# Residual sums on TensorE and LayerNorm statistics on ScalarE beside a clipped recurrence

## The reference

```python
h = ln(x, g1, b1);  real, imag = split(h @ W_to.T)
def step((sr, si), (r, i)):                 # 1024 steps, one after the other
    sr = sr * decay + r * 0.1;  si = si * decay + i * 0.1
    nr = clip(sr * c - si * s, -10, 10);  ni = clip(sr * s + si * c, -10, 10)
x2 = x + 0.1 * (scan_out @ W_from.T)
y  = x2 + 0.1 * (gelu(ln(x2, g3, b3) @ W1.T + b1) @ W2.T + b2)
x  = norm(y)                                                     # "layer 2" below
x  = norm(x + softmax(q(x) k(ctx)^T / 4) v(ctx) @ Wo.T + bo)     # "layer 3", 16 heads, 154 keys
```

## Time and profile before

| | us |
|---|---|
| median of 3 runs | 2178.86 (2178.73 to 2180.55) |
| the profiled execution's own time | 2181.41 |
| its span, first to last instruction | 2179.6 |
| last recurrence step ends | 603 |
| the stage of the change ends | 693 |

### The profile page before, as it was taken

How to read it: one execution, slowest core, us unless ns; L and a number is a source line. 1 busy time by engine, 2 the same in 40 slices (tenths; PEclk the granted TensorE clock), 3 DMA queues, 4 the chain that set the end, 5 groups by cost and what they waited for, 6 DMA issues and landing times.

```text
span 2179.6 us, 34541 instructions
## 1 busy us (share of the span) xinstructions
PE 1758.3 (81%) x12713; PEld 1265.2 (58%) x12713; DVE 1469.8 (67%) x5012; ACT 992.0 (46%) x2312; POOL 500.8 (23%) x602
## 2 busy tenths in 40 slices
PE   3546666766677877999999999999888999998808
PEld 1335555655564335566666766666657999983306
DVE  3788887787822587677777567776735666753695
ACT  2524334443343753455555345555315445543762
POOL 3011112111120012333333333333302333320002
PEclk9767788878787986999999999999999999999959
DMA  5000000000000011100000000000403333310001
GB/s 153 1 0 1 1 1 1 1 1 1 1 1 1 1 39 24 60 1 1 1 1 1 1 1 2 1 1 2 128 1 88 88 88 78 70 30 0 0 0 39
DMA packets 86314, 49.82 MB, mean 23 GB/s; under 512 B 40205, under 2 KB 83905, under 8 KB 85953
## 3 DMA queue, kind: packets, MB, share of 16 engines
q1 hardware_dynamic: 79361, 47.05, 8.3%
q10 hardware_dynamic: 6784, 0.56, 0.3%
HBM read 45.50 MB, written 2.10 MB: 22 GB/s over the span
## 4 chain that ended last, share of the span: by engine, by line
PE 60%; DVE 19%; ACT 9%; issue 3%; POOL 3%; POOLq 0%; DVEq 0%; ACTq 0%
PE PS L1526 6%; PE PS L1553 6%; PE PS L1824 5%; PE PS L1540 5%; PE PS L713 3%; PE PS L1511 3%; PE PS L1501 3%; DVE sq L667 3%; DVE nx L664 3%; PE PS L719 3%; PE PS L2237 3%; PE PS L1887 2%; PE PS L1568 2%; PE PS L1843 2%; PE PS L1493 2%
## 5 line engine op out<-in xcount | busy, mean ns | idle before, releaser
L1680 POOL TENSOR_SCALAR px<-px,crl 128x128 f32<-128x128 f32 (+7 forms) x128 | 225.9, 1765 | 420.6 <-DVE crl L1652 420.6
L1591 ACT ACTIVATE px<-PS,cnm 128x128 f32<-128x128 f32 (+7 forms) x256 | 189.5, 741 | 265.3 <-DVE cnm L1637 258.5
L182 POOL TENSOR_SCALAR rstd<-mv 128x1 f32<-128x1 f32 x128 | 41.5, 325 | 794.3 <-DVE mv L161 793.6
L667 DVE TENSOR_SCALAR sq<-nx 128x4 f32<-128x4 f32 x1024 | 186.0, 182 | 35.3 <-DVE nx L664 0.2
L664 DVE TENSOR_TENSOR_SCAN nx<-sq 128x6 f32<-128x6 f32 x1024 | 176.2, 172 | 35.5 <-SPq L2304 2.3
L1634 DVE TENSOR_REDUCE cm<-PS 128x1 f32<-128x128 f32 (+6 forms) x224 | 154.2, 689 | 56.9 <-PE PS L1526 56.4
L1540 PE MATMUL PS<-ident,px 128*128 128x128 f32 x1152 | 159.8, 280 | 13.3 <-ACT qT L1579 9.6
L1540 PEld LDWEIGHTS PS<-ident,px 128*128 128x128 f32 x1152 | 131.2, 142 | 60.6 <-issue 35.3
L1526 PE MATMUL PS<-kT,qT 64*128 64x512 f32 (+3 forms) x768 | 158.9, 519 | 4.5 <-ACT px L1591 2.6
L1553 PEld LDWEIGHTS PS<-pT,V 128*64 128x64 f32 x2304 | 124.1, 137 | 64.0 <-issue 34.6
L1553 PE MATMUL PS<-pT,V 128*64 128x128 f32 x2304 | 154.1, 278 | 6.4 <-DVE pT L1645 2.8
(11 more groups left out here) (318 smaller groups left out, 3830.3 us busy)
## 6 DMA issues: line engine op xcount, KB each, us to landing
xbs<-in_fside_Bx16xSxS SPq DMA_DIRECT2D x8, 1232.0 KB, 6.6
fsrc<-in_fside_Bx16xSxS SPq DMA_DIRECT2D x8, 1232.0 KB, 6.6
xmk<-in_mask_Bx16xSxS_bk SPq DMA_DIRECT2D x8, 308.0 KB, 8.5
fsrc<-in_mask_Bx16xSxS_bk SPq DMA_DIRECT2D x8, 308.0 KB, 8.3
X<-in_x SPq DMA_DIRECT2D x1, 2048.0 KB, 11.8
w<-in_L_attn_W_ffn SPq DMA_DIRECT2D x2, 1024.0 KB, 11.9
t<-in_L_ffn_w SPq DMA_DIRECT2D x2, 1024.0 KB, 11.3
out<-xs SPq DMA_DIRECT2D x16, 128.0 KB, 1.7
```

Of the source, the lines that this page charges most:

```text
L667: e.tensor_scalar(o, bass.AP(k.nx, 2, [[6, P], [0, 2], [3, 2]]), 10.0, -10.0, ALU.min, ALU.max).then_inc(sem("rec.clip"), 1)
L1591: e.activation(k.px[n % 2][:, h, 0:width], src, ACT.Exp, scale=-1.0, bias=k.cnm[:, n % 4, h:h + 1], accum_out=k.cl[:, n % 4, h:h + 1]).the ...
L1680: e.tensor_scalar(k.px[n % 2][:, 0, 0:width], k.px[n % 2][:, 0, 0:width], k.crl[:, n % 4, 0:1], None, ALU.mult).then_inc(sem("c.normal0"), 1)
```

## The change

For L = 1 and 2 in blocks 0 to 6, and for L = 3 in blocks 0 to 5 (`aside`), VectorE has no part in the norm any more. TensorE adds the residual by one more matmul into the same PSUM tile, with the identity, or ten times the identity where ScalarE scales the sum by 0.1 afterwards (`ident10`). ScalarE copies the sum from PSUM to `r4` and accumulates it (`sum`), forms the negative mean (`mean`), squares the deviations and accumulates them (`square`); GpSimd forms the reciprocal root from that (`root`), and ScalarE forms the shift and applies both (`shift`, `side`). The last blocks take the path of the other layers: residual, statistics and the application (`unit`) on VectorE. The numbers between the steps change: for L1 and L2 the step `shift` comes 7 and the turn 11 recurrence steps behind `sum`, where the turn came 7 behind `r`; for L3 it is 16 and 4. GpSimd's two additions to X move from the residual and the down steps to the turn and the up steps. Shown without unchanged lines; the new tiles and their reservation are left out.

```diff
...
+def aside(L, T):
+    return T % BT < {1: BT - 1, 2: BT - 1, 3: BT - 2}.get(L, 0)
+def taken(k, L, T):
+    return ("ln.act", k.ln_act["sum", L, T]) if aside(L, T) else ("ln.r", k.order.at("r", L, T))
...
     def unit(L, T):
-        if L == 0:
+        if L in (0, 1):
-        dst = k.xs4[:, lane, :] if L in (0, 7) else k.xt(T)
+        dst = k.xs4[:, lane, :] if L in (0, 1, 7) else k.xt(T)
...
-    def shift(L, T):
-        rs = k.rstd[:, lane_of(L, T), :]
-        w.wait_ge("ln.rstd", at("aggr", L, T))
-        e.tensor_scalar(rs[:, 0:1], k.mv[:, lane_of(L, T), 0:1], rs[:, 1:2], -1.0, ALU.mult, ALU.mult).then_inc(sem("ln.shift"), 1)
-    return {"aggr": aggr, "shift": shift}
+    def root(L, T):
+        s, rs, n = k.lst[:, lane_of(L, T), :], k.rstd[:, lane_of(L, T), :], 2 * at("root", L, T)
+        w.wait_ge("ln.act", k.ln_act["square", L, T])
+        e.tensor_scalar(rs[:, 0:1], s[:, 2:3], 1.0 / D, 1e-5, ALU.mult, ALU.add).then_inc(sem("ln.root"), 1)
+        w.wait_ge("ln.root", n - 1)
+        e.tensor_tensor(rs[:, 1:2], rs[:, 0:1], k.neghalf[:, :], ALU.pow).then_inc(sem("ln.root"), 1)
+    return {"aggr": aggr, "root": root}
...
     def turn(L, T):
-        if L in (1, 2):
+        if aside(L, T):
...
 def norm_scalar(e, w, k):
+    def total(L, T):
+        lane, b, t = lane_of(L, T), T // BT, T % BT
+        if L == 3:
+            n = at("n.query", T)
+            w.wait_ge("n.out", n)
+            ps = k.PS[:, 2 + n % 2, D:2 * D]
+        else:
+            if L == 1:
+                w.wait_ge("net.from", at("from", 1, t))
+            else:
+                w.wait_ge("net.down", at("down", 1, t))
+            ps = k.PS[:, 0, b * D:(b + 1) * D]
+        e.activation(k.r4[:, lane, :], ps, ACT.Identity, scale=1.0 if L == 3 else 0.1, accum_out=k.lst[:, lane, 0:1]).then_inc(sem("ln.act"), 1)
+    def mean(L, T):
+        s, n = k.lst[:, lane_of(L, T), :], k.ln_act["sum", L, T]
+        w.wait_ge("ln.act", n)
+        e.mul(s[:, 1:2], s[:, 0:1], -1.0 / D).then_inc(sem("ln.act"), 1)
+    def square(L, T):
+        n, lane = at("square", L, T), lane_of(L, T)
+        w.wait_ge("ln.act", k.ln_act["mean", L, T])
+        w.wait_ge("ln.act", k.ln_junk[n - 1])
+        e.activation(k.ljunk[:, :], k.r4[:, lane, :], ACT.Square, bias=k.lst[:, lane, 1:2], accum_out=k.lst[:, lane, 2:3]).then_inc(sem("ln.act"), 1)
+    def shift(L, T):
+        s, rs = k.lst[:, lane_of(L, T), :], k.rstd[:, lane_of(L, T), :]
+        w.wait_ge("ln.root", 2 * at("root", L, T))
+        e.mul(s[:, 3:4], s[:, 1:2], rs[:, 1:2]).then_inc(sem("ln.act"), 1)
     def side(L, T):
-        w.wait_ge("ln.shift", at("shift", L, T))
+        w.wait_ge("ln.act", k.ln_act["shift", L, T])
-        e.activation(dst, k.r4[:, lane, :], ACT.Identity, scale=k.rstd[:, lane, 1:2], bias=k.rstd[:, lane, 0:1]).then_inc(sem("ln.side"), 1)
+        e.activation(dst, k.r4[:, lane, :], ACT.Identity, scale=k.rstd[:, lane, 1:2], bias=k.lst[:, lane, 3:4]).then_inc(sem("ln.side"), 1)
...
-    return {"side": side, "put": put}
+    return {"sum": total, "mean": mean, "square": square, "shift": shift, "side": side, "put": put}
...
-        needs["n.query", T] = [("put", 2, T)] + ([("r", 3, k.near_tiles[n - 2])] if n > 1 else [])
+        needs["n.query", T] = [("put", 2, T)] + ([("sum" if aside(3, k.near_tiles[n - 2]) else "r", 3, k.near_tiles[n - 2])] if n > 1 else [])
-        needs["r", 3, T] = [("n.out", T)]
+        needs["sum" if aside(3, T) else "r", 3, T] = [("n.out", T)]
...
     def norm(L, gap):
-        for kind, wait in (("r", gap), ("stats", 0), ("aggr", 0), ("shift", 0), ("side", 5), ("turn", 2), ("put", 0)):
+        beside = (("sum", gap), ("mean", 0), ("square", 0), ("root", 0), ("shift", 7), ("side", 0), ("turn", 4))
+        alone = (("r", gap), ("stats", 0), ("aggr", 0), ("unit", 0), ("turn", 0))
+        for kind, wait in (*(beside if aside(L, t) else alone), ("put", 0)):
...
+            w.wait_ge("ln.side", at("side", 2, T - 1))
...
-        e.matmul(k.PS[:, 0, b * D:(b + 1) * D], k.zs[:, b, :], k.wfT[:, :], start=True, stop=True).then_inc(sem("net.from"), 1)
+        y = e.matmul(k.PS[:, 0, b * D:(b + 1) * D], k.zs[:, b, :], k.wfT[:, :], start=True, stop=not aside(1, t))
+        if aside(1, t):
+            w.wait_ge("tails", 2)
+            y = e.matmul(k.PS[:, 0, b * D:(b + 1) * D], k.ident10[:, :], k.xt(b * BT + t), start=False, stop=True)
+        y.then_inc(sem("net.from"), 1)
...
     def down(b, t):
-            m = e.matmul(k.PS[:, 0, b * D:(b + 1) * D], k.hT[:, j, b, :], k.W2T[:, j, :], start=j == 0, stop=j == 7)
+            m = e.matmul(k.PS[:, 0, b * D:(b + 1) * D], k.hT[:, j, b, :], k.W2T[:, j, :], start=j == 0, stop=j == 7 and not aside(2, t))
+        if aside(2, t):
+            w.wait_ge("net.bias", at("down", b, t))
+            m = e.matmul(k.PS[:, 0, b * D:(b + 1) * D], k.ident10[:, :], k.xt(b * BT + t), start=False, stop=True)
...
+        e.mul(k.ident10[:, :], k.ident[:, :], 10.0).then_inc(sem("tails"), 1)
...
-    def r(L, T):
+    def turn(L, T):
-            w.wait_ge("ln.r", at("r", L, T))
+            w.wait_ge(*taken(k, L, T))
-    def down(b, t):
-        w.wait_ge("net.added", at("down", b, t))
-        e.tensor_tensor(k.xt(b * BT + t), k.xt(b * BT + t), k.b2s[:, :], ALU.add).then_inc(sem("net.bias"), 1)
-    return {"tern_round": tern_round, "rec_in": rec_in, "r": r, "down": down}
+    def up(t, b):
+        if b < B:
+            w.wait_ge("net.added", at("down", b, t))
+            e.tensor_tensor(k.xt(b * BT + t), k.xt(b * BT + t), k.b2s[:, :], ALU.add).then_inc(sem("net.bias"), 1)
+    return {"tern_round": tern_round, "rec_in": rec_in, "turn": turn, "up": up}
...
 def near_ends(T):
-    yield 20, ("r", 3, T)
-    yield 1, ("stats", 3, T)
-    yield 1, ("aggr", 3, T)
-    yield 0, ("shift", 3, T)
-    yield 6, ("side", 3, T)
+    if aside(3, T):
+        for kind, wait in (("sum", 16), ("mean", 0), ("square", 0), ("root", 0), ("shift", 4), ("side", 0)):
+            yield wait, (kind, 3, T)
+    else:
+        for kind, wait in (("r", 20), ("stats", 0), ("aggr", 0), ("unit", 0)):
+            yield wait, (kind, 3, T)
...
-            w.wait_ge("ln.r", at("r", 3, k.near_tiles[n - 3]))
+            w.wait_ge(*taken(k, 3, k.near_tiles[n - 3]))
...
-            y = e.matmul(PS[:, 2 + n % 2, D:2 * D], k.nyT[:, c, :], k.x0T["Wo"][:, c, :], start=c == 0, stop=c == DC - 1)
+            y = e.matmul(PS[:, 2 + n % 2, D:2 * D], k.nyT[:, c, :], k.x0T["Wo"][:, c, :], start=c == 0, stop=c == DC - 1 and not aside(3, T))
+        if aside(3, T):
+            w.wait_ge("n.offset", n)
+            y = e.matmul(PS[:, 2 + n % 2, D:2 * D], k.ident[:, :], k.xt(T), start=False, stop=True)
...
-        if n > 2:
-            w.wait_ge("ln.side", at("side", 3, k.near_tiles[n - 3]))
+        if aside(3, T - 1):
+            w.wait_ge("ln.side", at("side", 3, T - 1))
...
-        for t in range(BT):
-            for b in range(B):
-                for L in (1, 2):
-                    k.room["turn", L, b * BT + t] = (0, "ln.r", k.order.at("r", L, BT + t))
...
+        k.ln_act, k.ln_junk, acts = {}, [0], 0
+        for step in k.order.steps:
+            if step[0] in ("sum", "mean", "square", "shift"):
+                acts += 1
+                k.ln_act[step] = acts
+                if step[0] == "square":
+                    k.ln_junk.append(acts)
+        for t in range(BT):
+            for b in range(B):
+                for L in (1, 2):
+                    k.room["turn", L, b * BT + t] = (0, *taken(k, L, BT + t))
```

More of the change, by code:

```diff
@@ L822, in near_tiles @@
     k.ny = sb("ny", [P, D], scope=sc)
+    k.ljunk = sb("ljunk", [P, D], BF16, scope=sc)
+    k.ident10 = sb("ident10", [P, P], scope=sc)
     k.nyT = sb("nyT", [P, DC, P], scope=sc)
@@ L2363, in build @@
         k.rstd = sb("rstd", [P, LANES, 2])
+        k.lst = sb("lst", [P, LANES, 4])
         k.ctxT = sb("ctxT", [P, DC, B * S2])
```

## The result

The changed kernel takes 2194.21 us (median of four runs, 2192.07 to 2194.58); the kernel before, beside it, 2179.7 (2178.73 to 2181.13). The ratio is 1.0063 [1.0051, 1.0075]: slower by 14.5 us, where the prediction had +8.2. The profiled execution took 2193.93, its span is 2192.1.

What follows compares the result with a forecast made beforehand. One loop over all engines bounds the kernel, 69.9 us a chunk. Links sum to +1.6 (71.5); 6 x 1.6 - 0.7 - 0.7 = +8.2 on 2181.4 gives 2189.6 profiled, 2187 as median; range 2180 to 2201.

Steps and rivals of the forecast that it cites:

- VectorE is the limit: Rival: VectorE bounds the chunk, so its removed work and waits, 9.9 us a chunk, all count: -61, 2118 us; chance 0.07.
- TensorE keeps its full clock: Rival: shorter gap ahead of `top` keeps TensorE at full clock; chunk 67.8, -14 in all, 2165 us; chance 0.17.
- the links cancel: Rival: (b) at 4.6 and (c) at +0.1 leave the chunk at 69.9 us, kernel 2178; chance 0.19.
- half clock and a late L2 turn: Rival: half clock in (c) and L2's late turn add 1.2 and 1 us a chunk: +21, 2200; no separate chance.
- (a): Loop from end of `top` to end of `from`: 13.0 us before, 13.9 with two identity matmuls, 0.9 together.
- (b): Loop from `from` to end of `side`: 5.4 us against 5.3 before, bounds 4.6 and 6.4; `side` ends at 19.3.
- (c): Loop to second tile's `peak`, three ups ahead instead of two: 25.8 us against 24.9 before, later by 0.9.
- (d): Loop from `peak` to the downs: one up fewer, but `nyT` behind gelu's table load; later by 0.55 us.
- (f): Loop from `normal` to `top`: first tile's residual, statistics and aggregate leave VectorE, -0.75 us.
- The first chunk: First chunk with a network, VectorE the limit: eight more steps eat most of the relief, -0.7 us.
- Behind the last chunk: End of stage: about -1.7 us for `unit` on VectorE, +1.0 for one more table change: -0.7.
- The table load for squares: Rival: `Square` on ScalarE causes table loads in L1 and L2, +8 to +12 over forecast, 2195 to 2199; chance 0.07.

Runs made afterwards that it cites:

- experiment 1: Changed kernel without the identity matmuls, so the residuals are left out and its output is not the reference's: 2168.22 us, ratio 0.9952, chunk 68.7.
- experiment 8: Changed kernel plus nine unread 128x128 matmuls a chunk, five ahead of L1's turn, four ahead of the first up: 2179.12 us, ratio 0.999.
- experiment 7: Changed kernel with the old list of 71 steps (shift 5 and turn 2 behind): 2196.54 us, ratio 1.0072, chunk 73.3.
- experiment 4: Kernel before, arithmetic unchanged, with side 9 and turn 6 steps behind instead of 5 and 2, list 16 steps longer: 2247.23 us, ratio 1.0314.
- experiment 9: Changed kernel with first tile's maxima 10 steps earlier, mix and normal kept in place, and 40 unread matmuls a chunk in TensorE's gaps: 2162.74 us, ratio 0.9925.
- experiment 12: Changed kernel with first tile's maxima 10 steps earlier, unread matmuls in TensorE's gaps, and second tile's normal, back and out 10 steps later: 2168.5 us, ratio 0.9948.
- The fastest kernel seen: Kernel before with first tile's maxima 10 steps earlier, mix and normal kept in place, and 34 unread matmuls a chunk in TensorE's gaps: 2157.5 us, ratio 0.9893.

## Why the prediction was right, and where its terms were off

**The mechanism.** One loop over all engines, in which VectorE's relief turns into waits ahead of `nrl` and of the second tile's maxima. That stands: 9.1 us a chunk against the 9 to 11 forecast. `top` to `top` is 71.95 against 71.5, but this closeness is luck: four of the pieces below are off by 0.5 to 2.2 us, and the errors cancel. Of the sign and the place of the waits the prediction can claim credit, of the size only in part: +14.5 against +8.2. "VectorE is the limit" fell, and so did "TensorE keeps its full clock" and "the links cancel". Of "half clock and a late L2 turn" the first half came; the late turn did not show, since VectorE waits for nothing at the first tile's `top`.

**The links**, in the chunk from 466.42 us:
(a) `from` ends at 480.47, 14.05 after `top` (forecast 13.9). (b) `side` ends at 485.55, 19.1 (19.3). Not by the way I summed: behind `from` the chain runs over the last `out` part and `nyS` to the shift, the 0.6 that I had called covered. (c) `peak` at 494.21, 27.8 (25.8; before 24.9). I had weighed full clock, 24.3, against half, 27, and taken a value between them. It was half, under the last scores too (0.83 us where I had 0.4). **This is the mis-sized term: +2.9 on `peak` where +0.9 was forecast.** Experiments 1 and 8 price the clock between the first up and `peak` at 3.0 us, where it doesn't fall elsewhere in its place. (d) `peak` to the downs 11.5 against 13.2 before: forecast +0.55, measured -1.7. Half of this is clock: `peak` itself takes 0.91 at 2.4 GHz where it took 1.72 at 1.2 in the earlier trace rows. For the other half, I had put `nyT` behind gelu's table load; the chain has `nyT` at 500.21 and the load behind it, so `out` runs beside the load. From `nyT` to the downs it is 5.5, before 6.4. (e) Downs 8.03 (8.1).
(f) `normal` to `top` took 20.81, before 20.83; forecast -0.75. Between the downs and `normal` lie 3.5, before 3.9, where VectorE's residual and statistics of L2 stood on the path; I had no term for this. The links make 27.8 + 11.5 + 8.0 + 3.5 + 20.8 = 71.6 for this chunk. Against the forecast (c) is off by +2.0, (d) by -2.2, (f) by +0.75 and the piece without a term by -0.45: about nothing in all. What is left over in the mean of 71.95 is in other chunks (70.7 to 73.9). In the two longest (72.3 and 73.9) `from` with its identity matmuls runs at the low clock as well and ends 16.4 us or more behind `top`, in place of 14.05.

**Why (f) gave nothing**, and why VectorE was rid of 1.7 a chunk, not 5 (work without waits: 69.94 - 5.3 = 64.6 before, 71.95 - 9.1 = 62.9 after). Two reasons stand in the time lines. The first, in the kernel before, is the tile's residual, statistics and aggregate:
```profile
376.00 0.16 DVE L664 TENSOR_TENSOR_SCAN nx<-sq 128x6 f32<-128x6 f32 x1
...
376.27 0.42 DVE L157 BATCH_NORM_STATS2 st<-r 128x6 f32<-128x256 f32 x1
376.61 0.15 DVE L664 TENSOR_TENSOR_SCAN nx<-sq 128x6 f32<-128x6 f32 x1
...
376.88 0.18 DVE L161 BATCH_NORM_AGGREGATE mv<-st 128x2 f32<-128x6 f32 x1
377.00 0.17 DVE L664 TENSOR_TENSOR_SCAN nx<-sq 128x6 f32<-128x6 f32 x1
```
A scan follows the one before after 0.41 us. With the statistics between them it is 0.61: an instruction of 0.42 costs 0.20, since it starts while its neighbour still runs. The three add 0.43 to their steps (0.25 at `r`, 0.20, and -0.02), not the 0.8 that I had added up from busy times. Where nothing overlaps them, as for the pair at `r`, it is 0.7 to 0.8 a tile. For a chunk that is 2 x 0.43 + 4 x 0.76 = 3.9.

The second is GpSimd. VectorE of the changed kernel, then GpSimd in the same time:
```profile
483.99 0.73 DVE L712 TENSOR_SCALAR sq<-nx 128x4 f32<-128x4 f32 x1
484.76 0.65 DVE L709 TENSOR_TENSOR_SCAN nx<-sq 128x6 f32<-128x6 f32 x1
485.45 0.65 DVE L712 TENSOR_SCALAR sq<-nx 128x4 f32<-128x4 f32 x1
486.13 0.65 DVE L709 TENSOR_TENSOR_SCAN nx<-sq 128x6 f32<-128x6 f32 x1
...
519.94 0.57 DVE L709 TENSOR_TENSOR_SCAN nx<-sq 128x6 f32<-128x6 f32 x1
```
```profile
483.98 1.41 POOL L843 TENSOR_TENSOR X<-X,r 128x256 f32<-128x256 f32 x2
485.34 1.41 POOL L848 TENSOR_TENSOR X<-X,b2s 128x256 f32<-128x256 f32 x2
486.71 0.72 POOL L1113 TENSOR_TENSOR X<-X,x0bo 128x256 f32<-128x256 f32 x1
...
519.75 0.73 POOL L1113 TENSOR_TENSOR X<-X,x0bo 128x256 f32<-128x256 f32 x1
```
Steps of 0.17 take 0.57 to 0.73 as long as GpSimd adds 128x256 tiles, and 0.17 again when it has ended. From 120 to 620 us the changed kernel has 45 such instructions, 20.1 us over 0.17 in all; the kernel before has 21 and 8.3. GpSimd does the same six additions a chunk in both; before, some of them lay beside maxima and statistics, now all lie beside the recurrence. In the six chunks that is 2.9 us a chunk against 1.2. So 3.9 - 1.7 = 2.2 of relief should be left, and 1.7 was measured. Most of it falls where VectorE waits afterwards; the 0.40 at 519.94 is inside (f), and it eats the 0.43. The Trainium skill ("SBUF — State Buffer", "SBUF: two separate sides") has VectorE and GpSimd share a port pair that one of them locks for a whole instruction, against a VectorE operation with two SBUF inputs when GpSimd reads SBUF too. The Trainium skill names a second case in that place, an operation in a two-port mode. The scans agree with the first; the clip has one tensor from SBUF and is held as well, and whether that is the second case, no run here shows. No run took GpSimd's additions away, so the cause is read from the coincidence in time. One run comes near to an experiment: in experiment 7, with the same arithmetic, these additions fall where VectorE waits. Its six chunks have 10 such lengthened steps in place of 37, and VectorE's work is 60.5 us a chunk in place of 62.9.

**The first chunk**: forecast -0.7, measured +1.1. The eight steps cost 3.3; its four longer steps beside GpSimd cost 2.0 against 1.2; four tiles, two pairs of 1.42 and 1.60 us, bring back only 3.0. Sum +1.1.

**Behind the last chunk**: forecast -0.7, measured +1.6. The first up and `peak` again run at half clock there (the first up takes 1.71 us in the chain from 630.71 us), and the downs begin 40.5 after the last `top` in place of 37.9; 1.0 comes back later; one place is L2's turn, ahead of which TensorE stands 3.0 us for `unit` on VectorE, before 4.42 for ScalarE.

**The table load for squares** fell. ScalarE's groups, 60 to 712 us:
```profile
L253 ACT ACTIVATE ljunk<-r,lst 128x256 bf16<-128x256 f32 x40 | 20.1, 502 | 2.0 <-ACT ljunk L253 0.4
L810 ACT ACT_TABLE_LOAD x15 | 19.2, 1283 | 0.3
L1045 ACT ACT_TABLE_LOAD x15 | 19.2, 1283 | 0.3
L242 ACT ACTIVATE r<-PS 128x256 f32<-128x256 f32 x40 | 15.1, 380 | 30.8 <-PE PS L754 20.5 <-PE PS L772 8.1 <-PE PS L1009 2.3
L242 ACT ACTIVATION_READ_ACCUMULATOR r<-PS 128x1 f32 x40 | 8.0, 201 | 0.1
```
40 squares and 30 loads, two more than before, all at gelu and the exponential: by the rule that the prediction cited from the Trainium skill ("ScalarE: Activation LUTs", "Table sets: the hidden batching unit") square behaves as the functions that it names as filler. A change of table took 1.3 us here (load at 500.49, gelu at 501.79), not the 2.66 that the prediction quotes. Squares took 0.50, within the 0.45 to 0.65 named, sums 0.38, below it.

**What stays open.** How much of a chunk the list's eight steps alone would cost with the norms left on VectorE: experiment 4 has 16 and took 10.3 for them, and nothing says how that divides. Where in a chunk TensorE's clock falls: in experiment 1, and in every other chunk of experiment 8, the low stretch moved to other instructions and didn't go. And what keeps experiments 9 and 12 from going under 67: the wait moves between `nrl` and the first tile's maxima, by an amount near the ten steps that were shifted, which says that VectorE's list and the second layer's chain are both close behind.

## What to carry to other kernels

Price what an engine is rid of by the pitch of what it does meanwhile, not by busy times: independent instructions overlap, and those of a neighbour engine can lengthen them. When a loop runs over in-order engines, an engine that is relieved only moves its waits; distances in the list (35 steps to 25: 10 us of the kernel, with no arithmetic changed) and TensorE's clock in short gaps were worth more here than the split of work. Look at single chunks when an edit touches the clock: a mean of 69.9 was made of 68.4 and 71.5. The fastest kernel seen, 2157.5, has no part of the change.

## What the runs showed of the hardware

Nine small matmuls a chunk, with nothing to compute, made the kernel 15 us faster (2194.2 to 2179.1): four instructions of 256 columns took 2.04 us at 1.2 GHz and 1.10 at 2.4. In every other chunk the low clock came back 17 us earlier, under other matmuls, and took the gain again. An identity matmul on 256 columns cost 0.43 of its own, and taking out all of them 3.25 a chunk, most of it by the clock of other matmuls. VectorE's instructions of 6 elements last 0.65 in place of 0.17 us while GpSimd adds 128x256 tiles in SBUF. A sum from PSUM with its accumulator read takes 0.38 + 0.20 us on ScalarE and the read overlaps by half.
